# First group's variance 1 by adding transfers and DRAM instead of eight one-column matmuls

## The reference

```
x1, x2 = x[:, :F], x[:, F:]
h1 = leaky_relu(layer_norm(x1 @ W1.T));  h2 = leaky_relu(layer_norm(x2 @ W1.T))   # 256 wide
h1 = leaky_relu(layer_norm(h1 @ W2.T));  h2 = leaky_relu(layer_norm(h2 @ W2.T))   # 64 wide
h  = leaky_relu(layer_norm(concat([h1, h2]) @ W3.T))                              # 8 wide
y  = h @ W4.T                                                                     # 1 wide
```

## Time and profile before

| | us |
|---|---|
| median of 3 runs (lowest, highest) | 237.54 (236.88, 237.69) |
| profiled execution, whole time | 237.35 |
| its span | 235.6 |
| PE busy in it | 227.2 |
| DVE busy | 194.6 |
| ACT busy | 152.9 |
| POOL busy | 7.9 |

### The profile page before, as it was taken

The page is one execution under the profiler, slowest core; times in us unless marked ns, Lnnn a source line. Parts: engine busy times, 40 slices in busy tenths (PEclk is TensorE's granted clock), DMA queues, the critical chain, the costliest instruction groups (busy, mean ns, idle before and its releaser), DMA issues.

```text
span 235.6 us, 2891 instructions
## 1 busy us (share of the span) xinstructions
PE 227.2 (96%) x1022; PEld 181.4 (77%) x1022; DVE 194.6 (83%) x246; ACT 152.9 (65%) x242; POOL 7.9 (3%) x16
## 2 busy tenths in 40 slices
PE   7999999999999999999999999999999999999992
PEld 2687777888888777887778887888888888888772
DVE  1679999979889999996669499999989899949424
ACT  5797989689496596973667318546555577515630
POOL 1000000000000000000000310000000000000004
PEclk9999999999999999999999999999999999999998
DMA  5999978877867577657624444688584705050000
GB/s 193 373 416 412 390 268 274 265 225 271 273 224 250 200 237 222 226 173 223 259 88 115 164 170 178 189 273 330 192 267 163 271 14 178 0 178 4 0 0 1
DMA packets 13550, 47.99 MB, mean 204 GB/s; under 512 B 1888, under 2 KB 2272, under 8 KB 11744
## 3 DMA queue, kind: packets, MB, share of 16 engines
q1 hardware_dynamic: 13536, 47.81, 58.5%
HBM read 47.80 MB, written 0.00 MB: 203 GB/s over the span
## 4 chain that ended last, share of the span: by engine, by line
PE 63%; DVE 20%; ACT 7%; issue 3%; DMA 3%; SPq 2%; POOL 1%; POOLq 0%; DVEq 0%; ACTq 0%
PE acc L886 58%; DVE xe_lo L608 5%; DVE xt_lo L608 3%; DMA xe_raw<-x 3%; ACT xe_hi L491 2%; DVE x_sum L661 2%; DVE we_lo L625 2%; PE acc L1008 2%; PE acc L1021 2%; ACT xt_hi L491 2%; DVE xr_lo L608 1%; ACT unused L445 1%; DVE ws_lo L616 1%; DVE x_sum L666 1%; ACT we_hi L451 1%
## 5 line engine op out<-in xcount | busy, mean ns | idle before, releaser
L886 PE MATMUL acc<-xe_lo,we_hi 128*128 128x512 f32 x176 | 68.9, 392 | 0.7 <-DVE xe_lo L608 0.6
L886 PE MATMUL acc<-xe_hi,we_lo 128*128 128x512 f32 x176 | 68.5, 389 | 0.0
L491 ACT CAST xe_hi<-xe_raw 128x1024 fp32r<-128x1024 f32 (+1 forms) x47 | 47.9, 1026 | 29.9 <-PE acc L886 25.0
L608 DVE TENSOR_TENSOR xe_lo<-xe_raw,xe_hi 128x1024 fp32r<-128x1024 f32 (+1 forms) x47 | 55.5, 1199 | 12.7 <-ACT xe_hi L491 12.7
L886 PE MATMUL acc<-xe_hi,we_hi 128*128 128x512 f32 x176 | 48.4, 391 | 0.3 <-DVE stage L710 0.3
L886 PEld LDWEIGHTS acc<-xe_lo,we_hi 128*128 128x128 f32 x176 | 33.0, 188 | 9.0 <-issue 2.3
L886 PEld LDWEIGHTS acc<-xe_hi,we_hi 128*128 128x128 f32 x176 | 32.8, 188 | 7.6 <-issue 1.0
L886 PEld LDWEIGHTS acc<-xe_hi,we_lo 128*128 128x128 f32 x176 | 33.0, 188 | 6.7
L491 ACT CAST xt_hi<-x_sum 128x2048 fp32r<-128x2048 f32 x14 | 26.8, 1911 | 16.0 <-DVE x_sum L671 16.0
L608 DVE TENSOR_TENSOR xt_lo<-x_sum,xt_hi 128x2048 fp32r<-128x2048 f32 x14 | 32.0, 2289 | 1.9 <-ACT xt_hi L491 1.9
L886 PE MATMUL acc<-xt_lo,ws_hi 128*128 128x512 f32 x64 | 25.0, 391 | 0.0
(11 more groups left out here) (98 smaller groups left out, 249.6 us busy)
## 6 DMA issues: line engine op xcount, KB each, us to landing
xe_raw<-x SPq DMA_DIRECT2D x51, 512.0 KB, 4.3
xs_raw<-x SPq DMA_DIRECT2D x14, 1024.0 KB, 5.2
stage<-w SPq DMA_DIRECT2D x21, 256.0 KB, 5.0
xe_raw<-x SPq DMA_DIRECT2D x2, 256.0 KB, 3.4
stage<-w SPq DMA_DIRECT2D x2, 128.0 KB, 2.9
w_raw<-w SPq DMA_DIRECT2D x1, 64.0 KB, 3.9
w_sb<-w SPq DMA_DIRECT2D x1, 8.0 KB, 3.7
w_sb<-w SPq DMA_DIRECT2D x1, 16.0 KB, 3.8
```

The lines of the kernel that those rows point to most:

```text
L491: act.copy(hi_of(u, part), raw_of(u, part)).then_inc(hi_ready[part.buffer], 1)
L608: dve.tensor_tensor(lo_of(u, part), raw_of(u, part), hi_of(u, part).bitcast(F32), ALU.subtract)\
L886: return pe.matmul(acc[:, bank, :], w, x, start=first, stop=True, skip_group_check=True)
```

## The change

The eight matmuls of sum_variance1 for the first group are gone from PE. POOL waits for both sums of squares and folds the 128 partitions in seven transfers that add into their target: 64 rows onto 64, then 32 onto 32, down to 1 onto 1, each 1024 columns wide (sq1_rows is sq1_sum of both b, side by side in stage). The one row left is stored to a DRAM tensor var1_rows, and four transfers load it back into var1 with the rows of x on the partitions, 128 x 2 single elements each. Every one but the last three waits for the one before it.

VectorE's variance1 at the crossing is gone. Only the two copies into small stay there. Reciprocal, variance2, layer3, layer4 and finish of the first group move from the run with n.nth = 6 to the run with n.nth = SEVEN + 4 = 10 (unit 30), behind a wait for the four loads. SP issues the two late weight loads in the run of unit 30 (n.n + 4) instead of unit 26 (n.n + 8), and waits for the store first, since one of them overwrites sq1_rows. Bank P6 is waited for by drained. The counts of var1_summed and var1_copied in the second group's tail are lowered to match.

```diff
@@ buffers
+        sq1_rows = stage[:, 2 * NC:4 * NC]
+        var1_rows = nc.dram_tensor("var1_rows", (B * NC,), F32, kind="Internal").ap()
@@ SP
-                if n and n.n + 8 == W_WORK[len(FIRST)].n:
+                if n and n.n + 4 == W_WORK[len(FIRST)].n:
                     sp.wait_ge(h3_summed, B)
+                    sp.wait_ge(var1_stored, 16)
                     for i in range(len(FIRST), len(W_WORK)):
                         load_w(i)
@@ POOL, before consts_ready and the powers
+            pool.wait_ge(sq1_summed, B)
+            for k in range(7):
+                w = P >> (k + 1)
+                if k:
+                    pool.wait_ge(var1_folded, 16 * k)
+                pool.dma_start(sq1_rows[0:w, :], sq1_rows[w:2 * w, :], accum_op=ALU.add).then_inc(var1_folded, 16)
+            pool.wait_ge(var1_folded, 16 * 7)
+            pool.dma_start(var1_rows.rearrange("(o n) -> o n", o=1), sq1_rows[0:1, :]).then_inc(var1_stored, 16)
+            pool.wait_ge(var1_stored, 16)
+            for b in range(B):
+                rows = var1_rows[(1 - b) * NC:(2 - b) * NC].rearrange("(h t p) -> t p h", h=H, t=T)
+                for t in range(T):
+                    pool.dma_start(var1[:, b * J + t * H:b * J + (t + 1) * H], rows[t],
+                                   allow_slow_non_contiguous=True).then_inc(var1_landed, 16)
@@ VectorE, variance1
-                dve.wait_ge(var1_copied, n - 1)
+                dve.wait_ge(var1_copied, n)
@@ VectorE, the run's end
                 if crosses(es):
-                    variance1(B, 0, B, var1_ps(0, 0, B))
                     dve.wait_ge(h3_summed, B)
                     dve.wait_ge(var2_summed, B)
                     dve.tensor_copy(small[:, 0:B * J], var2_ps(0, 0, B))
                     dve.tensor_copy(small[:, B * J:B * J + B * J * N3], h3_ps(0, 0, B)).then_inc(small_copied, 1)
+                first_end = n.nth == SEVEN + 4
+                if first_end:
+                    dve.wait_ge(var1_landed, 16 * B * T)
+                    step(dve.reciprocal(var1_inverse[:], var1[:]))
                     dve.wait_ge(small_copied, 1)
                     variance2(B, 0, B, small[:, 0:B * J])
                 w_lo(after[0])
                 lo(after[0], after[0].parts[0])
-                if crosses(es):
+                if first_end:
                     layer3(1, 0, B, small[:, B * J:B * J + B * J * N3])
                     layer4(0, B)
                 lo(after[0], after[0].parts[1])
-                if crosses(es):
+                if first_end:
                     finish(1, 0, 0, B)
@@ VectorE, the second group's tail
-            variance1(B * g + 1, 0, 1, var1_ps(g, 0, 1))
+            variance1(1, 0, 1, var1_ps(g, 0, 1))
-            variance1(B * g + 2, 1, 2, var1_ps(g, 1, 2))
+            variance1(2, 1, 2, var1_ps(g, 1, 2))
@@ PE, free
                     if bank == P6:
-                        pe.wait_ge(var1_copied, g)
+                        pe.wait_ge(drained, 5 * (g - 1) + 1)
@@ PE, behind unit 20
                     for b in range(B):
                         layer2(u.g - 1, b, range(M))
-                    for b in range(B):
-                        sum_variance1(u.g - 1, b)
```

More of the change, by code:

```diff
@@ L262, in rec_kernel @@
         var1_summed = sem("var1_summed")
+        var1_folded = sem("var1_folded")
+        var1_stored = sem("var1_stored")
+        var1_landed = sem("var1_landed")
         var2_summed = sem("var2_summed")
```

## The result

The changed kernel takes 235.2 us, median of 5 runs (235.05 to 235.75); the kernel before, with its runs beside these, 237.54. The ratio is 0.9896, 95% interval 0.9856 to 0.9937. In two later comparisons on other chips it was 0.9903 (0.9878 to 0.9929) and 0.9923 (0.9911 to 0.9936). The forecast was 235.6. The profiled execution took 235.2, its span is 233.4.

The account below looks back on a forecast made before the run. PE, busy 96% of the span, was taken as the bound: 396 matmuls without a wait run to the end. Saving 1.80 + 0.15 = 1.95 us from 237.35 gives 235.40, plus 0.19 for the median: 235.6 us, range 235.0 to 236.3.

Parts of the forecast that it names:

- Step 1: At PE's crossing, removing sum_variance1's 16 one-column matmul records saves 1.80 us (1.70 to 1.95).
- Step 2: At the first unit after the crossing's seven, PE's 0.15 us stall goes because VectorE's detour leaves the crossing.
- Step 3: Banks P6 and P7 are free before PE asks for both at 132.3, so PE doesn't wait.
- Step 4: POOL's transfer chain takes 37 us, landing at 156 (bounds 133 to 169), hidden with 14 us of cover.
- Step 5: VectorE's detour, moved to 170.63, stays hidden: xt_lo ends 0.78, 0.75 and 0.73 us before PE needs it.
- Step 6: The two late weight loads, issued at 177.7, land at 182.7; ScalarE centres them from 182.59, with 2.1 us of cover.
- A: Transfers land too late for VectorE behind nth 10's xt_lo; adding costs double, time 246.5; 13% together with A2.
- A2: Same place as A: running VectorE instructions hold POOL's issue, stall 12 us, time 247.6; 13% together with A.
- B: VectorE's margin in step 5 is overrun by a slower power or POOL's work; 236.4 to 237.4 us; 9%.
- C: Nothing gained: POOL's queue adds work at the program's start or end, outside the span; 237.3 us; 6%.

Follow-up runs that it names:

- e1: Changed kernel with the first group's sum_variance1 matmuls, reciprocal and copy kept at the crossing, no POOL transfers, only the later work moved: 237.43 us, ratio 1.0005.
- e6: Changed kernel with the seven folds as plain copies of the same size, without the addition: 235.6 us in one execution.
- e4: Changed kernel with the first group's end two seven-units later, at nth 12 (unit 34): 236.8 us, ratio 0.9978.
- e3: Changed kernel with the first group's end two seven-units earlier, at nth 8 (unit 26): 243.22 us, ratio 1.0241.
- e5: Changed kernel with the first group's variance 2 also taken off PE by POOL transfers, 30 transfers instead of 12: 237.67 us, ratio 1.0014.
- e8: e5 with the first group's end one seven-unit later (nth 11, unit 32) and layer3 behind both xe_lo: 235.34 us, ratio 0.9923.
- e10: e8 with 16 increments of an unused semaphore put behind PE's warm-up matmuls: 235.58 us, ratio 0.9920.
- e2: Changed kernel without its twelve POOL transfers, the first group's var1 set to 1.0 by POOL: 235.9 us, ratio 0.9933.
- e7: Changed kernel with the first group's end one seven-unit earlier, at nth 9 (unit 28): 235.6 us, median of 10 runs, ratio 0.9931.

## Why the prediction was right

- **Step 1**, the matmuls: 1.80 predicted (1.70 to 1.95), 1.80 measured at the crossing. The share that needs them gone, by e1, is 1.79. Starting long matmuls behind layer 2 costs no more than behind the one-column ones did (four of them in 1.20 us against 1.18).
- **Step 2**, the stall at the first seven-unit: 0.15 predicted, 0.16 measured, alone in e1 and in the changed kernel (90.07 to 89.91). It goes with the move whatever PE does.
- **Step 3**, the banks: no wait of PE behind the crossing in the changed kernel.
- **Step 4**, the chain: 37 us to a landing at 156 predicted; 39.8 and 159.3 measured, and 37.7 to 42.9 us over the traces with this chain. The 3.7 us for a transfer was a fair mean by luck, since the reason given, a small size, is not what decides: landings ran from 2.1 to 6.1 us, with the longest at 64 KB and not at 256, and the addition, put at nothing, costs 3 to 8 us of the seven folds. It cost PE nothing, since the place of the user leaves 10.8 us. The rule of the Trainium skill that I set beside it ("DMA: Bandwidth & Descriptors", "Anatomy of one DMA — SWDGE (gpsimd) path"), 2 us fixed and the bytes at 436 GB/s, gave a landing near 145, 14 us before the measured one. The trace doesn't agree: the seven adding folds took 4.1 us each in the mean, beside loads of x. e6's plain folds of 128 and 64 KB, which no 1 MB load overlaps, took what it gives (2.3 and 2.1 us).
- **Step 5**, VectorE's margin: 0.78, 0.75 and 0.73 predicted, 1.07, 1.05 and 1.03 measured. The mis-sized term is the start of unit 30's xt_lo: I moved it with PE, to 168.43, but in the kernel before VectorE was still catching up with PE there: its xt_lo came every 9.13 us up to 170.38 and the next 9.88 later, while a pair of units takes PE 10.2, which is also the distance in the changed kernel (157.69 to 167.90). It came at 167.90; 0.2 of the difference is the execution's earlier crossing, 0.3 is this. e4 shows what this margin is worth: with the detour two units later it is overrun, and PE waits.
- **Step 6**, the weight loads: issued at 176.59 (177.7 predicted), ScalarE centres them at 182.51 (182.59), nobody waits for them.
- **Rivals.** A's price is shown by e3 and e5: the DMA wait, less the margin, lands on PE. Its place and condition were right; only its point from which it decides, 52 us of chain, was not reached with 40, and an adding transfer does not cost double. A2: POOL's issues beside VectorE's tensor_tensor rows took 0.76 to 0.81 us (1.06 the first, with 64 rows), each began 0.3 us after the landing before it, whatever VectorE ran, and xt_lo takes 2.29 in both kernels. That agrees with what the Trainium skill, "SBUF — State Buffer", "Who interferes with whom", says of tensor_tensor. B did not occur. C did not occur here. The 0.65 us at the end of e5, e8 and e10 has C's place. Twelve transfers on POOL's queue don't bring it, as the changed kernel beside e2 shows; whether thirty do was not tested.

The sum was right on the traces to a hundredth of a us, which is closer than its terms were known (1.70 to 1.95 for the first alone); to that digit it is luck, the two terms themselves are not. The median came 0.4 under the forecast; 0.2 of this is seen ahead of the crossing in the profiled executions, and in the two later comparisons the distance of the medians was 2.04 (237.32, 235.28) and 1.93 (237.28, 235.35), not 2.34.

## What to carry to other kernels

On a kernel whose main engine runs without a wait to the end, a piece of work taken off that engine was worth its own length, however slow the way that replaced it: 1.8 us of PE gave way to 40 us of dependent transfers at no cost to PE. What has to be worked out are two dates, not a sum: when the result is asked for against when it lands, and how much the engine that now uses it can be late; the place of the user has a limit on both sides (e3 and e4). The landing has to be taken with its spread, three us or more here (e7). And when a further gain of the same kind is shown by the trace and missing in the time (e8), compare the ends of the traces before looking for a cost in the middle.

One thing was read in the code: VectorE multiplies the sum for variance 2 by 1/var1 and then by var1, and var1 is used nowhere else. So the value of variance 1 drops out of what follows, but for rounding, and a version that never computes it needs neither matmuls nor transfers. e2 is such a version for the first group: with var1 at 1.0 nothing is left out of the output in effect, and its stretch is 99.14 as well. The gain of this change could be had without its chain of 40 us; only the second group, whose matmuls stay, was not tried without them.

## What the runs showed of the hardware

- Adding transfers issued by POOL, SBUF to SBUF, from 256 KB to 4 KB, beside loads of x: 2.1 to 6.5 us from issue to landing, with 0.8 us of issue (1.06 for 64 rows); plain ones 1.8 to 5.3, with 0.5 us of issue (0.71). The first, of 256 KB, took 4.1 to 4.3 with the addition and 3.0 without. The fold that was issued just behind the 1 MB load near 128 us was the slowest of the seven in each trace with these folds (6.0 to 6.3 us, without the addition 5.3).
- A load of 256 single 4-byte elements: 0.72 to 0.77 us of issue on POOL, 3.1 to 4.6 to landing in the changed kernel and 2.4 to 5.5 over all traces.
- The same chain of twelve transfers took 37.7 to 42.9 us from the first issue to the last landing in six traces.
- The power on POOL takes 2.51 us for 8 columns and 1.01 for 4, beside VectorE's work.
- The end of PE's own program set the end of the span in e5, e8 and e10, 0.65 us later than elsewhere (2.66 us instead of 2.01 from the start of y's last instruction), after the output had landed; from what it comes is not known.
